# Masking and folding the softmax maxima another way in two attention layers of a four-layer Trainium2 kernel

## The reference, cut to what matters

```
q, k, v = heads of xn @ Wq + bq, xn @ Wk + bk, xn @ Wv + bv        (layer 3: q, k turned by rope)
scores  = q . k / 4        (layer 0: + slope[h] * (key - 511); -inf where key > query)
probs   = softmax(scores over the keys)
out     = (probs @ v) @ Wo + bo
```

## Time and profile before

| | |
|---|---|
| median of 3 runs | 1648.97 us (1645.29 to 1654.58) |
| the profiled execution | 1639.4 us, its span 1638.1 us |
| PE busy | 1399.5 us, 85% |
| DVE busy | 1005.6 us, 61% |
| ACT busy | 654.0 us, 40% |
| POOL busy | 411.3 us, 25% |
| mean granted TensorE clock | 0.904 of full speed |

### The profile page before, as it was taken

How to read it: one execution, slowest core, us unless ns; L and a number is a source line. 1 busy time by engine, 2 the same in 40 slices (tenths; PEclk the granted TensorE clock), 3 DMA queues, 4 the chain that set the end, 5 groups by cost and what they waited for, 6 DMA issues and landing times.

```text
span 1638.1 us, 18683 instructions
## 1 busy us (share of the span) xinstructions
PE 1399.5 (85%) x7204; PEld 821.9 (50%) x7204; DVE 1005.6 (61%) x1854; ACT 654.0 (40%) x930; POOL 411.3 (25%) x399
## 2 busy tenths in 40 slices
PE   1588989989999877699758999999789889889886
PEld 0355655656566544355326767766335335335333
DVE  6875575555555898876388353357775765655651
ACT  3333453444545653256113242230353453352352
POOL 2443141231211142121274132142213302302300
PEclk9969999899889987799759999999699988889989
DMA  7000000000023000016333000003101000100100
GB/s 221 7 1 1 1 1 1 1 1 1 20 62 139 10 26 26 1 49 184 115 98 32 1 1 0 1 9 74 38 0 35 19 1 1 52 1 1 52 1 13
DMA packets 32009, 53.10 MB, mean 32 GB/s; under 512 B 5456, under 2 KB 19760, under 8 KB 31280
## 3 DMA queue, kind: packets, MB, share of 16 engines
q1 hardware_dynamic: 27840, 40.99, 8.1%
q0 software_dynamic: 4080, 10.92, 3.1%
HBM read 43.89 MB, written 10.52 MB: 33 GB/s over the span
## 4 chain that ended last, share of the span: by engine, by line
PE 42%; DVE 15%; ACT 4%; issue 3%; POOL 2%; DMA 1%; SPq 0%; DVEq 0%; POOLq 0%
PE pair L610 17%; PE bank L610 14%; DVE max L1088 4%; PE bank L686 3%; ACT probs L1577 2%; PE pair L673 2%; POOL gathered L1932 1%; PE pair L643 1%; PE pair L653 1%; DMA gathered<-outbox,slots 1%; DVE qs L1104 1%; DVE mix_h L1496 1%; PE pair L664 1%; DVE conv L1177 1%; DVE normed L1248 0%
## 5 line engine op out<-in xcount | busy, mean ns | idle before, releaser
L1088 DVE TENSOR_REDUCE max<-pair 128x2 f32<-128x1024 f32 (+3 forms) x256 | 251.5, 1017 | 116.6 <-PE pair L656 64.0
L1577 ACT ACTIVATE probs<-pair 128x1024 f32<-128x1024 f32 (+3 forms) x256 | 209.8, 867 | 203.0 <-PE pair L676 123.8
L1890 POOL TENSOR_TENSOR h_low<-hidden,h_high 128x512 fp32r<-128x512 f32 x64 | 82.4, 1294 | 278.0 <-ACT h_high L1612 277.8
L673 PE MATMUL pair<-qs,ks 52*128 52x512 f32 (+3 forms) x512 | 116.6, 479 | 26.4 <-DVE max L1088 13.4
L653 PE MATMUL pair<-ks,qs 50*128 50x512 f32 (+3 forms) x512 | 121.7, 486 | 20.2 <-DVE max L1088 16.0
L686 PE MATMUL bank<-probs,v 128*32 128x512 f32 (+3 forms) x1024 | 130.8, 587 | 3.9 <-ACT probs L1577 3.1
L610 PE MATMUL pair<-wqk,xnT 128*128 128x512 f32 x192 | 101.4, 654 | 14.4 <-DVE cut_low L1026 10.8
L673 PEld LDWEIGHTS pair<-qs,ks 52*128 52x128 f32 x512 | 50.0, 203 | 122.8 <-issue 40.1
L1129 DVE TENSOR_TENSOR x<-bank,x 128x512 f32<-128x512 f32 x32 | 22.0, 688 | 119.4 <-PE bank L610 119.4
L653 PEld LDWEIGHTS pair<-ks,qs 50*128 50x128 f32 x512 | 52.7, 205 | 77.5 <-DVE max L1088 33.1
L1950 POOL TENSOR_TENSOR h<-mix_h,h 128x512 bf16<-128x512 f32 x48 | 55.3, 1165 | 128.5 <-DVE mix_h L1496 102.1
(11 more groups left out here) (295 smaller groups left out, 2856.0 us busy)
## 6 DMA issues: line engine op xcount, KB each, us to landing
expert_in<-in_experts_in SPq DMA_DIRECT2D x16, 352.0 KB, 4.3
expert_out<-in_experts_out SPq DMA_DIRECT2D x16, 256.0 KB, 4.8
h<-comb SPq DMA_DIRECT2D x4, 1024.0 KB, 5.3
x<-in_x SPq DMA_DIRECT2D x4, 512.0 KB, 10.3
wqk<-in_wqk SPq DMA_DIRECT2D x4, 512.0 KB, 3.6
tern_raw<-in_ffn_in SPq DMA_DIRECT2D x8, 256.0 KB, 6.8
inbox<-zeros SPq DMA_DIRECT2D x4, 512.0 KB, 5.4
tokens<-inbox SPq DMA_DIRECT2D x16, 128.0 KB, 2.2
```

What stands on the lines that cost most here:

```text
L673: made = mm(to[:, hh, q0:T], m.ks[g % 2][r0:r0 + AUG + 4, p, kt * P:(kt + 1) * P], m.qs[g % 2][r0:r0 + AUG + 4, p, q0:T], start=True, stop ...
L1088: V.tensor_reduce(m.max[:, g % 2, p, qt, :], to[:, :, 0:n], AX.X, ALU.max).then_inc(*s.done("top"))
L1577: A.activation(m.probs[(2 * kt + p) % 4][:, :, q0:T], to[:, :, q0:T], ACT.Exp).then_inc(*s.done("exp"))
L1890: Q.tensor_tensor(m.h_low[k][:, j, :], m.hidden[k][j % 2][:, :], m.h_high[k][:, j, :].bitcast(F32), ALU.subtract).then_inc(*s.done("low"))
```

## The change

The maxima go into the query half of `stack` itself, columns 50 and 51; PE turns that half a second time (`refold`, in place of `lift`), and ACT copies it over `qs` (`refolded`, in place of DVE's `lifted`). `max_cols` goes. `cut` now waits for `refold` of the group two before it, since that reads the same stack.

In layer 0 the mask products of `score` go. `top` runs, for each of the two heads, one tensor_tensor_reduce that adds the mask (now 128 x 512, zeros and the diagonal block), writes the scores back to PSUM and takes the maximum; in the program it stands as two rows, the main one and one that writes the accumulator. Layer 3's `top` stays one TENSOR_REDUCE. The mask of `prob` is added by four products with 64 rows each instead of two with 128.

```diff
     def score(k, b, g, p, qt):
...
-            made = mm(to[:, hh, 0:n], m.qs[g % 2][r0:r0 + AUG + 2, p, qt * P:(qt + 1) * P], m.ks[g % 2][r0:r0 + AUG + 2, p, 0:n], start=True, stop=k == 3)
-        if k == 0:
-            for hh in PAIRS:
-                made = mm(to[:, hh, n - P:n], m.ident16[:, :], m.mask_qk[:, :], start=False, stop=True)
+            made = mm(to[:, hh, 0:n], m.qs[g % 2][r0:r0 + AUG + 2, p, qt * P:(qt + 1) * P], m.ks[g % 2][r0:r0 + AUG + 2, p, 0:n], start=True, stop=True)
         made.then_inc(*s.done("score"))
+    def masked(blocks, mask):
+        for part in PAIRS:
+            for hh in PAIRS:
+                rows_ = slice(STACK * hh, STACK * hh + STACK)
+                made = mm(blocks[:, hh, part * STACK:(part + 1) * STACK], mask[rows_, part, :], m.ident16[rows_, :], start=False, stop=part == 1)
+        return made
-    def lift(k, b, g):
...
+    def refold(k, b, g):
+        to = bank("refold", k, b, g)
         pe.wait_ge(*at("shift", k, b, g))
+        for tt in range(TT):
+            for p in PAIRS:
+                made = turn(to[:, p, tt * P:(tt + 1) * P].bitcast(F32R), m.stack[g % 2][:, tt, 0, 2 * p:2 * p + 2, :].rearrange("p h r -> p (h r)"), m.ident_r[:, :])
...
     def prob(k, b, g, kt, p):
...
         if k == 0:
-            for hh in PAIRS:
-                made = mm(to[:, hh, q0:q0 + P], m.ident16[:, :], m.mask_kq[:, :], start=False, stop=True)
+            made = masked(to[:, :, q0:q0 + P], m.mask_kq)
...
     def cut(k, b, g):
...
-            dve.wait_ge(*at("fold", k, b2, g2, 0))
             dve.wait_ge(*at("fold", k, b2, g2, 1))
+            dve.wait_ge(*at("refold", k, b2, g2))
...
     def top(k, b, g, p, qt):
...
-        V.tensor_reduce(m.max[:, g % 2, p, qt, :], to[:, :, 0:n], AX.X, ALU.max).then_inc(*s.done("top"))
+        if k == 3:
+            V.tensor_reduce(m.max[:, g % 2, qt, 2 * p:2 * p + 2], to[:, :, :], AX.X, ALU.max).then_inc(*s.done("top"))
+            return
+        dve.wait_ge(*s.cast_landed())
+        for hh in PAIRS:
+            scores, h = to[:, hh, 0:n], 2 * p + hh
+            V.tensor_tensor_reduce(scores, scores, m.mask_qk[:, T - n:T], 1.0, NEG, ALU.add, ALU.max, m.max[:, g % 2, qt, h:h + 1]).then_inc(*(s.done("top") if hh else dve.up()))
     def shift(k, b, g):
...
+        top_, cols = m.max[:, g % 2, :, :], m.stack[g % 2][:, :, 0, :, AUG + 2:AUG + 4]
+        V.tensor_scalar(cols[:, :, :, 0], top_, -1.0, None, ALU.mult).then_inc(*dve.up())
+        dve.wait_ge(*dve.own())
+        V.scalar_tensor_tensor(cols[:, :, :, 1], top_, -1.0, cols[:, :, :, 0].bitcast(F32), ALU.mult, ALU.subtract).then_inc(*s.done("shift"))
-    def lifted(k, b, g):
-        to, qs = bank("lift", k, b, g), m.qs[g % 2]
-        dve.wait_ge(*at("lift", k, b, g))
-        V.tensor_tensor(qs[:, :, :], to[:, :, :], qs[:, :, :].bitcast(F32), ALU.add).then_inc(*s.done("lifted"))
...
+    def refolded(k, b, g):
+        to = bank("refold", k, b, g)
+        act.wait_ge(*at("refold", k, b, g))
+        A.copy(m.qs[g % 2][:, :, :], to[:, :, :]).then_inc(*s.done("refolded"))
...
-    "unit": "16 17 30 31 52 53 57 59 89 90 141 142 165 166 171 172 204 205 256 257 280 281 286 287 319 320 346 347 372 373 398 399 630 631 635 636 640 641 645 646 651 652 658 659 662 663 666 667 672 673 684 685 688 689 692 693 698 699 709 710 714 715 718 720",
+    "unit": "14 15 17 18 20 21 23 24 55 56 58 59 61 62 64 65 193 194 196 197 199 200 202 203 312 313 315 316 318 319 321 322 631 632 634 635 637 638 640 641 649 652 664 666 668 670 672 673 677 680 681 683 684 687 688 690 698 702 713 716 718 720 722 723",
```

More of the change, by code:

```diff
@@ L55 @@
         "turn": keys(ALL, B), "qkv": keys(HEADS, B, range(TT)), "fold": keys(HEADS, B, range(G), PAIRS),
-        "score": keys(HEADS, B, range(G), PAIRS, range(TT)), "lift": keys(HEADS, B, range(G)),
+        "score": keys(HEADS, B, range(G), PAIRS, range(TT)), "refold": keys(HEADS, B, range(G)),
         "prob": keys(HEADS, B, range(G), range(TT), PAIRS), "weigh": keys(HEADS, B, range(G), range(TT)),
@@ L71 @@
         "cut": keys(HEADS, B, range(G)), "top": keys(HEADS, B, range(G), PAIRS, range(TT)), "shift": keys(HEADS, B, range(G)),
-        "lifted": keys(HEADS, B, range(G)), "headed": keys(HEADS, B, range(G)), "joined": keys(ALL, B, PAIRS),
+        "headed": keys(HEADS, B, range(G)), "joined": keys(ALL, B, PAIRS),
         "gated": keys((0, 2), B, range(UNITS)), "mean_out": keys(B), "fed": keys(B, PAIRS),
@@ L84 @@
         "tern_cast": keys(range(12)), "turned": keys(ALL, B),
-        "folded": keys(HEADS, B, range(G), PAIRS), "exp": keys(HEADS, B, range(G), range(TT), PAIRS), "summed": keys(HEADS, B, range(G)),
+        "folded": keys(HEADS, B, range(G), PAIRS), "refolded": keys(HEADS, B, range(G)), "exp": keys(HEADS, B, range(G), range(TT), PAIRS), "summed": keys(HEADS, B, range(G)),
         "rowed": keys((0, 1, 3), B), "tanh": keys((0, 2), B, range(UNITS)), "high": keys((0, 2), B, range(UNITS)), "square": keys(B, range(UNITS)),
@@ L301 @@
 PLACES = {"pair": ((0, 1), (2, 3), (4, 5)), "acc": ((6,),), "one": ((7,),), "two": ((6,), (7,))}
-BANKS = {"tern_sum": "pair", "turn": "pair", "qkv": "pair", "fold": "pair", "score": "pair", "lift": "pair", "prob": "pair", "weigh": "acc", "back": "one",
+BANKS = {"tern_sum": "pair", "turn": "pair", "qkv": "pair", "fold": "pair", "score": "pair", "refold": "pair", "prob": "pair", "weigh": "acc", "back": "one",
          "rows": "pair", "unit": "pair", "down": "one", "mean": "one", "proj": "pair", "gate": "two", "gamma": "pair", "inflow_turn": "pair", "mem_turn": "two",
@@ L321 @@
     "score": lambda k, b, g, p, qt: [("top", (k, b, g, p, qt))],
-    "lift": lambda k, b, g: [("lifted", (k, b, g))],
+    "refold": lambda k, b, g: [("refolded", (k, b, g))],
     "prob": lambda k, b, g, kt, p: [("exp", (k, b, g, kt, p))],
@@ L652, in score @@
             r0 = hh * STACK
-            made = mm(to[:, hh, 0:n], m.qs[g % 2][r0:r0 + AUG + 2, p, qt * P:(qt + 1) * P], m.ks[g % 2][r0:r0 + AUG + 2, p, 0:n], start=True, stop=k == 3)
-        if k == 0:
-            for hh in PAIRS:
-                made = mm(to[:, hh, n - P:n], m.ident16[:, :], m.mask_qk[:, :], start=False, stop=True)
+            made = mm(to[:, hh, 0:n], m.qs[g % 2][r0:r0 + AUG + 2, p, qt * P:(qt + 1) * P], m.ks[g % 2][r0:r0 + AUG + 2, p, 0:n], start=True, stop=True)
         made.then_inc(*s.done("score"))
-    def lift(k, b, g):
-        to = bank("lift", k, b, g)
+    def refold(k, b, g):
+        to = bank("refold", k, b, g)
         pe.wait_ge(*at("shift", k, b, g))
-        for p in PAIRS:
-            for qt in range(TT):
-                made = turn(to[:, p, qt * P:(qt + 1) * P], m.max_cols[:, p, qt, :, :].rearrange("p h r -> p (h r)"), m.ident)
-        made.then_inc(*s.done("lift"))
+        for tt in range(TT):
+            for p in PAIRS:
+                made = turn(to[:, p, tt * P:(tt + 1) * P].bitcast(F32R), m.stack[g % 2][:, tt, 0, 2 * p:2 * p + 2, :].rearrange("p h r -> p (h r)"), m.ident_r[:, :])
+        made.then_inc(*s.done("refold"))
     def prob(k, b, g, kt, p):
         to = bank("prob", k, b, g, kt, p)
-        pe.wait_ge(*at("lifted", k, b, g))
+        pe.wait_ge(*at("refolded", k, b, g))
         q0 = kt * P if k == 0 else 0
@@ L681, in weigh @@
         pe.wait_ge(*at("v_out", k, b, kt))
-        pe.wait_ge(*at("exp", k, b, g, kt, 0))
-        pe.wait_ge(*at("exp", k, b, g, kt, 1))
+        for p in PAIRS:
+            pe.wait_ge(*at("exp", k, b, g, kt, p))
         q0 = kt * P if k == 0 else 0
@@ L928, in mix @@
         made.then_inc(*s.done("mix"))
-    parts = {"tern_sum": tern_sum, "turn": turn_x, "qkv": qkv, "fold": fold, "score": score, "lift": lift, "prob": prob, "weigh": weigh, "back": back, "rows": rows, "out": out,
+    parts = {"tern_sum": tern_sum, "turn": turn_x, "qkv": qkv, "fold": fold, "score": score, "refold": refold, "prob": prob, "weigh": weigh, "back": back, "rows": rows, "out": out,
              "unit": unit, "down": down, "mean": mean, "proj": proj, "gate": gate, "gamma": gamma, "inflow_turn": inflow_turn, "mem_turn": mem_turn, "shared": shared,
@@ L1498, in vector_program @@
     parts = {"set_dve": set_dve, "tern_scaled": tern_scaled, "quarter": quarter, "half": half, "stat": stat, "norm": norm, "cut_low": cut_low, "biased": biased, "v_out": v_out,
-             "rope_a": rope_a, "rope_b": rope_b, "cut": cut, "top": top, "shift": shift, "lifted": lifted, "headed": headed, "joined": joined, "fed": fed, "gated": gated,
+             "rope_a": rope_a, "rope_b": rope_b, "cut": cut, "top": top, "shift": shift, "headed": headed, "joined": joined, "fed": fed, "gated": gated,
              "mean_out": mean_out, "conv": conv, "gate_out": gate_out, "norm_sum": norm_sum, "norm_inv": norm_inv, "flow": flow, "q_norm": q_norm, "scan": scan,
@@ L1810, in mix_tanh @@
         A.activation(m.mix_t[j % 2][:, :], to[:, 0, :], ACT.Tanh, scale=0.5).then_inc(*s.done("mix_tanh"))
```

(11 more changed lines are left out.)

18 lines of the change are left out of this document (5 added, 13 removed), and 280 rows, old and new, of the table DUE.

## The result

The changed kernel takes 1593.1 us (median of 4 runs, 1586.6 to 1595.9) against 1647.1 us before (1644.6 to 1654.6): a ratio of 0.966 with a 95% interval of 0.961 to 0.970. That is 54 us off; the forecast was 1605 us. The profiled execution has a span of 1590.1 us, 48.0 less than before.

A forecast was written before the change was run, and what follows sets the result against it. PE's work was taken to bound layer 0: -42 + 8 = -34 us, with -10 in layer 3, gives 1595 from 1639.4; the median lay 9.6 above, so 1605 us. Forecast's own range 1590 to 1620, whole range 1565 to 1662.

The forecast's parts named there:

- the middle: Stage between layer 0 and layer 3: holds no edited parts, forecast at nothing, give or take 8 us.
- the signs that were to show it right: Layer 0: PE busy about 40 us less, maxima 0.5 to 0.6 us per head, PE's waits for maxima 10 or 20 us.
- rival B: Layer 0: half-row `prob` masks near 0.4 us, lower clock more often; no gain, 1641 us; sign clock under 0.85; chance 0.18.
- (1): Layer 0 score masks leave PE: 128 pairs at 0.22 us each, 28 us off.
- (3): Layer 0 masks of `prob` as four half-row products: 0.16 us instead of 0.22, 128 times, 8 us off PE.
- Term (5): Layer 0 maxima on DVE: 8.7 us a group instead of 6.6, 34 us more, still under PE's 384.
- PE's work is what counts in layer 0: Layer 0: PE busy 426 of 460 us bounds it; DVE has 185 us to spare.
- Term (2): `lift` to `refold`: eight transposes take 0.67 us instead of 1.02, 5.6 us off PE in each of two layers.
- new waits: Layer 0, PE: 8 us charged, half a microsecond for each group.
- The new order: Layer 0: units no longer stand between groups, PE goes at DVE's pace after three scores; charged 8 us of waits.
- rival C: PE's losses to waits and clock shrink by 20 us with the order, `prob` masks give -14: about 1577 us; chance 0.20.
- Rival A: Layer 0 maxima run at the scan's rate, 15.5 us a group, decisive from about 14.3: slower, 1658 us; chance 0.14.

## Why the prediction was right, and where it was not

The sum came out: layer 0 -38.0 us where -34 was forecast, layer 3 -17.1 for -10, the middle +7.1 inside its 8, 1593 inside 1590 to 1620. But in layer 0 this is luck: its terms were far off and offset each other. Of the signs that were to show it right, PE's waits for maxima came (22.4 us), but its busy time from 60 to 520 us fell by 6 us and not by 40, and the clock went to 0.86, close to the 0.85 that was rival B's sign.

**Terms (1) and (3), PE's masks.** I priced a mask by its own rows, 0.22 us, and wrote that the products in different halves take twice one's columns. They don't: 0.43 us was the time to the full-array mask behind them, and the same trace of before has four such products in 0.57 us in layer 3, which I had not read. The terms were 44 us and not 28, and 30 and not 8 (I gave the latter a lower bound of -14). I had set the rows against the Trainium skill, TensorEngine Tiling (Array Packing), Key Properties. It says that different tiles can work in parallel and that a change of tiling mode drains TensorE. The trace agrees with both halves: 0.57 us for the four products, and 0.43 for two with a full-array product behind them.

**Term (5), the maxima.** They were to add 34 us to VectorE and nothing to the layer, because VectorE had 185 us to spare. The group takes 7.2 us; before, from start to start, it was 2 x (1.13 + 0.88 + 0.61 + 0.34) = 5.9. So 1.3 us for a group, 21 us: the size was too large. But with PE's work the same these 21 us cost 33, and putting them at nothing was wrong.

**The step that failed** is "PE's work is what counts in layer 0", with its waits for VectorE at 8 us and its clock unchanged. Three kernels that differ by one edit each, all in the new order with the second turn, show it in us at the median: both masks full on PE 1580, weights' mask in half rows 1567, the scores' mask then moved to VectorE 1593. The last step takes 44 us off PE and puts 21 on VectorE, and loses 26. Making VectorE's part 9.4 us a group longer lost 135 us, while giving PE the scores' mask as well lost 7. So VectorE's maxima count in time however idle it is on average. The old order shows this as well (1594 with the mask on PE in half rows, 1619 with it on VectorE); but there PE's work counts too, since the two half-row edits, some 60 us of it, brought 58. I charged 8 us for new waits; the changed kernel shows 17.6 us of them at `score` and 4.8 at `prob`, and the clock of 60 to 480 us is 0.85 where the kernel with the mask on PE has 0.94.

**Term (2) and layer 3.** I took the second turn for 5.6 us of PE's work in each layer. In the new order it is worth 30 us in layer 3; in layer 0 it gains 7 us with both masks full on PE (474.5 to 467.5) and loses 5 with the masks as changed. In layer 3 PE waits 13.6 us of the 30 for `lifted`, so more of the price was in the wait than in the transposes. Part of the 30 may be due to where I put `lifted`: against the kernel before, layer 3 gains 17.1.

**The new order** I charged with 8 us and gave no gain. Alone it gives 31 us. In the profiled executions that is 43.0 in layer 0, with the clock at 0.94 instead of 0.91, less 2.6 between and 12.7 in layer 3. My rival C, with 20 us for waits and clock, had this mechanism.

**Rival A** was to decide from 14.3 us of maxima for a group and to end at 1658, with 15.5 us. At 16.6 us the kernel takes 1728, and there is a loss long before: with PE's work the same, 5.9 to 7.2 us cost 33, and 7.2 to 16.6 cost 135. On a straight line between the last two (an estimate) the whole gain of 54 us would be gone at 11 us. That the change did not end slower is due to the instruction's speed (0.65 us for 512 columns and not the scan's 1.21) and to the order and the second turn, which pay for it.

What stays open: why the clock falls with the masked maxima. With PE's work the same and its idle time within 1 us it is 0.87 against 0.94; in the new order half-row score masks lowered it too (0.88 against 0.94 for full rows, 1574 against 1567 us, with intervals that overlap), while in the old order they raised it from 0.88 to 0.94. No run isolates the cause.
